# A graph attention kernel: three of sixteen tiles a chunk masked on VectorE after the exponential instead of on TensorE before it

## The reference

```python
e = (Wh @ a_src)[:, None] + (Wh @ a_dst)[None, :]
e = jnp.where(e > 0, e, ALPHA * e)             # ALPHA = 0.2
scores = jnp.where(adj > 0, e, NEG_BIG)        # -9e15 where there is no edge
attention = jax.nn.softmax(scores, axis=1)
h_prime = attention @ Wh
return jax.nn.elu(h_prime)
```

## Time and profile before

| what | value |
|---|---|
| median of 3 runs | 651.01 us (648.59 to 651.77) |
| profiled execution, its time | 648.58 us |
| profiled execution, its span | 646.5 us |
| TensorE busy | 569.7 us (88%), 3130 matmuls |
| VectorE busy | 361.8 us (56%), 490 instructions |
| ScalarE busy | 278.8 us (43%), 297 instructions |
| GpSimd busy | 31.9 us (5%), 28 instructions |
| mean granted TensorE clock | 0.952 |

### The profile page before, as it was taken

How to read it: one execution, slowest core, us unless ns; L and a number is a source line. 1 busy time by engine, 2 the same in 40 slices (tenths; PEclk the granted TensorE clock), 3 DMA queues, 4 the chain that set the end, 5 groups by cost and what they waited for, 6 DMA issues and landing times.

```text
span 646.5 us, 7470 instructions
## 1 busy us (share of the span) xinstructions
PE 569.7 (88%) x3130; PEld 195.1 (30%) x3169; DVE 361.8 (56%) x490; ACT 278.8 (43%) x297; POOL 31.9 (5%) x28
## 2 busy tenths in 40 slices
PE   5534999999999999999989998999769899999997
PEld 3301223333223344222233222245332222333332
DVE  2985766546766536766646766534989966000010
ACT  1573455434555432555532555335848666100000
POOL 0500000201000101000000000022000000000000
PEclk9556999999999999999998999999979999899999
DMA  8990000000000000000000000000000000000000
GB/s 358 368 399 11 1 0 2 1 0 1 2 1 0 1 0 3 0 1 2 0 1 1 1 0 2 0 2 1 0 1 0 2 1 0 1 1 0 1 0 33
DMA packets 3041, 19.33 MB, mean 30 GB/s; under 512 B 320, under 2 KB 320, under 8 KB 960
## 3 DMA queue, kind: packets, MB, share of 16 engines
q1 hardware_dynamic: 2864, 17.83, 6.8%
q10 hardware_dynamic: 144, 1.03, 0.5%
HBM read 18.33 MB, written 0.52 MB: 29 GB/s over the span
## 4 chain that ended last, share of the span: by engine, by line
PE 65%; DVE 21%; issue 5%; ACT 4%; DMA 2%; POOL 1%; POOLq 0%; DVEq 0%; ACTq 0%
PE PROD L653 14%; PE X L854 9%; PE S L665 9%; PE X L645 8%; PE PROD L854 7%; DVE X L1129 6%; DVE aB L1335 5%; ACT big L382 2%; DVE nadj L1238 2%; PE M L631 2%; PE X L545 2%; DMA big<-in_adjT 2%; PE S L869 2%; DVE big L1116 1%; POOL rr L319 1%
## 5 line engine op out<-in xcount | busy, mean ns | idle before, releaser
L382 ACT ACTIVATE big<-X,v 128x1024 f32<-128x1024 f32 x128 | 137.3, 1112 | 139.8 <-PE X L645 139.4
L1129 DVE SCALAR_TENSOR_TENSOR X<-wB,v,aB 128x1024 f32<-128x1024 f32 x128 | 161.5, 1289 | 59.3 <-ACT big L382 57.9
L653 PE MATMUL PROD<-big,Wh 128*64 128x512 f32 x512 | 125.9, 609 | 0.5 <-ACT big L382 0.2
L645 PE MATMUL X<-nadj,bigI 128*128 128x512 bf16 x233 | 67.3, 386 | 23.4 <-DVE X L1129 19.7
L665 PE MATMUL S<-big,onesf 128*32 128x512 f32 x512 | 68.2, 605 | 0.6 <-ACT big L382 0.6
L653 PEld LDWEIGHTS PROD<-big,Wh 128*64 128x64 f32 x512 | 30.2, 136 | 81.1 <-ACT big L382 49.8
L645 PEld LDWEIGHTS X<-nadj,bigI 128*128 128x128 bf16 x256 | 15.8, 97 | 95.8 <-DVE X L1129 72.6
L319 POOL TENSOR_TENSOR rr<-var,mhalf 128x8 f32<-128x8 f32 x8 | 17.3, 2161 | 371.5 <-DVE var L995 371.5
L854 PE MATMUL PROD<-nadj,Wh 128*64 128x512 f32 x128 | 30.3, 602 | 2.9 <-ACT nadj L473 2.9
L631 PE MATMUL M<-big,level 128*32 128x512 fp8e4 x256 | 19.8, 439 | 14.0 <-ACT big L421 11.7
L854 PE MATMUL PROD<-big,Wh 128*64 128x512 f32 x128 | 31.3, 606 | 0.7 <-ACT big L473 0.5
(11 more groups left out here) (266 smaller groups left out, 574.9 us busy)
## 6 DMA issues: line engine op xcount, KB each, us to landing
big<-in_adjT SPq DMA_DIRECT2D x13, 1024.0 KB, 7.9
aB<-in_adjT SPq DMA_DIRECT2D x3, 1024.0 KB, 8.8
cst<-in_cst ACTq DMA_DIRECT2D x1, 1008.5 KB, 5.6
x<-in_xT SPq DMA_DIRECT2D x1, 512.0 KB, 6.2
out<-x SPq DMA_DIRECT2D x2, 256.0 KB, 2.0
```

The source lines that it names most:

```text
L382: act.activation(prob[:, t % U, :], X[t % 2][:], ACT.Exp, bias=v2[l % 2][:, k:k + 1]).then_inc(p_ready, 1)
L645: last = pe.matmul(X[t % 2][:, hh * BANK:(hh + 1) * BANK], bigI[:], nadj[:, k, half_cols(c, hh)], start=False, stop=True, skip_group_check ...
L653: last = pe.matmul(PROD[c][feat(hh), :], Wh[l % 2][:, k, :], prob[:, t % U, hh * BANK:(hh + 1) * BANK], start=k == 0, stop=k == NB - 1)
L1129: dve.scalar_tensor_tensor(X[t % 2][:], wB[:, cols(c)], v8[l % 2][:, k:k + 1], aB[:, cols(c)], ALU.max, ALU.add).then_inc(x_written, 1)
```

## The change

In chunk 0 the tiles 4, 11 and 14, in chunk 1 the tiles 2, 7 and 12 of each layer (24 tiles in all) lose their `mask` on TensorE. Their exponential waits for the exponent (`x_written`) in place of the mask, and runs over unmasked values. Behind it VectorE limits the result to 3e38, multiplies it with the 8-bit adjacency and writes it back to the same buffer (`hide`, a new function, one instruction of 128x1024). In VectorE's list `hide` of tile k stands behind `exponents` of tile k+1. `products` of such a tile waits for a new semaphore, `p_hidden`, as well as for `p_ready`. Since the masks left out no longer count, `exponential` of the others waits for a number of `x_masked` that is lower by those left out so far (`hidden_by`).

```diff
+HIDE = ((4, 11, 14), (2, 7, 12))
+LARGE = 3.0e38
...
+        def hidden_by(l, c, k):
+            full = len(HIDE[0]) * (l + (1 if c else 0)) + len(HIDE[1]) * l
+            return full + sum(1 for h in HIDE[c] if h <= k)
...
             def exponential(l, c, k):
                 t = NB * (NCH * l + c) + k
-                act.wait_ge(x_masked, t + 1)
+                if k in HIDE[c]:
+                    act.wait_ge(x_written, t + 1)
+                else:
+                    act.wait_ge(x_masked, t + 1 - hidden_by(l, c, k))
...
             def mask(l, c, k):
                 t = NB * (NCH * l + c) + k
+                if k in HIDE[c]:
+                    return
                 pe.wait_ge(x_written, t + 1)
...
             def products(l, c, k):
                 t = NB * (NCH * l + c) + k
                 pe.wait_ge(p_ready, t + 1)
+                if k in HIDE[c]:
+                    pe.wait_ge(p_hidden, hidden_by(l, c, k))
...
+            def hide(l, c, k):
+                t = NB * (NCH * l + c) + k
+                dve.wait_ge(p_ready, t + 1)
+                dve.scalar_tensor_tensor(prob[:, t % U, :], prob[:, t % U, :], LARGE, adj[:, k, cols(c)], ALU.min,
+                                         ALU.mult).then_inc(p_hidden, 1)
...
                 for k in range(NB):
                     exponents(l, 0, k)
+                    if k - 1 in HIDE[0]:
+                        hide(l, 0, k - 1)
                     if 6 <= k < 10:
                         (target_first, target_second)[k % 2](l, 1, (k - 6) // 2)
...
                 for k in range(NB):
                     exponents(l, 1, k)
+                    if k - 1 in HIDE[1]:
+                        hide(l, 1, k - 1)
                     if k == 4:
                         reciprocals(l, 0)
```

More of the change, by code:

```diff
@@ L208, in program @@
         x_masked = sem("x_masked")
+        p_hidden = sem("p_hidden")
         p_ready = sem("p_ready")
```

## The result

The change makes the kernel slower: 661.39 us median (659.39 to 664.15, 4 runs) against 649.80 (648.31 to 651.77, the three runs of the table and a fourth); ratio 1.0182, 95% interval 1.0158 to 1.0207, that is +11.8 us (+10.3 to +13.5). The forecast was +10.1 us and 660, with a range of 652 to 667.

A forecast was written before the change was run, and what follows sets the result against it. TensorE was taken to set the pace, with the loop through ScalarE and VectorE nearly as long. Even tiles 0, tile 11 5.2 and tile 7 4.9 sum to +10.1 us: 660 us, range 652 to 667.

The forecast's parts named there:

- The bound: Attention tile pairs: TensorE sets the pace at 3.83 us; the loop through ScalarE and VectorE has 0.1 us to spare.
- Price of the hide: One 128x1024 hide on VectorE: 1.22 us, from the trace's fp32 operation within SBUF; 0.57 to 1.29 considered.
- rival (c): Hides on VectorE run at half throughput, 2.3 us each: +29 us, 680; chance 0.06.
- Even tiles: Chunk 0 tiles 4, 14, chunk 1 tiles 2, 12: saved mask becomes a wait for the next exponent; 0 us.
- Tile 11: Chunk 0, second of its pair: product waits for the hide, sums +1.3 us, four times, 5.2 us.
- Tile 7: Chunk 1: product waits for the hide; +1.5 us in layers 0 and 1, +0.95 in layers 2 and 3; 4.9 us.
- The sum: Whole kernel: the tile costs added together, +10.1 us, giving 660.
- (a): All 24 masks saved on TensorE, hides fit VectorE's idle time: 11.5 us less, 639.5; chance 0.10.
- the two points named: Exponent k+1 ending before products (needed 183.83, read 184.20); hide ending before its product is due (needed 182.89, read 184.13).
- (b): Even tiles save their masks after all, 7.7 us; odd tiles cost as forecast: +2.4, 653.4; chance 0.12.
- signs to look for: Profile after: 208 mask matmuls, 24 hides near 1.22 us, eight product waits, even pairs 3.83, chunk 0 +1.3 a layer.
- The granted clock: Should stay at 2.4 GHz, since it is 1.00 around the present TensorE wait of 1.31 us.

The follow-up runs named there:

- Experiment 4: Kernel after, the 24 masks left out and the hides too, so those tiles stay unmasked: 646.66 us, -3.0 us against the kernel before.
- Experiment 2: Kernel after with only tiles 4, 14 (chunk 0) and 2, 12 (chunk 1) hidden, first of their pairs: 647.82 us, -2.3 us against the kernel before.
- experiment 9: Kernel after with 36 tiles hidden, all first of their pair, TensorE's sums ahead of the one mask left: 639.03 us, -12.0 us against the kernel before.

## Why the prediction held, point by point

The forecast and its mechanism held. That 660 came so near 661.39 is in part luck: it was reckoned from 651.01, and the terms below are off in both directions.

**The bound.** TensorE looks full, but the ways through ScalarE and VectorE are as long. Experiment 4 shows that TensorE's own work is not the limit by itself (3.0 us back for 11.5 us of masks), and its timeline shows the two waits: for exponential 10 at a second tile, for exponent 15 at a first one.

**Price of the hide.** 1224 ns measured, 1.22 taken. With its 8-bit second source the hide takes as long as the fp32 operation L1352 of the earlier trace rows, 1224 ns as well. The half throughput of rival (c), about 2.3 us by the prediction's estimate, did not appear in any of the 24, which took 1215 to 1227 ns. The Trainium skill's "Vector Engine (DVE) Microarchitecture Reference", section 7, asks for it; this trace disagrees.

**Even tiles.** Forecast 0, at most 0.1 each. At tile 14 the trace has 0.43 us of waiting for the exponent where the mask was, and a pair of unchanged length. Tile 4 of layers 1 to 3 gives 0.2 us: the pair of products 2 and 3, where mask 4 stood, takes 3.65 for 3.83. Experiment 2 gives -2.3 (-3.6 to -1.0), more than those three times 0.2.

**Tile 11.** Forecast +1.3, measured +1.46 in each of the four layers. The terms that were short: from the hide's end to product 11 it is 0.14 us and not 0.05, and product 11 to mask 12 takes 1.01 and not 0.93, which was half of a pair's 1.87.

**Tile 7.** Forecast +1.5 and +0.95, measured +1.46 and +0.87, twice each.

**The sum.** 4 x 1.46 + 2 x 1.46 + 2 x 0.87 = 10.5, less 3 x 0.2 at tile 4, is 9.9; forecast 10.1. Two misses cancel here: 0.16 too little at tile 11 in each of four layers, and tile 4 put at nothing. The profiled spans differ by 12.7. From the first product to the start of the last pair of layer 3 the trace grows by 10.7 (365.65 to 376.38); of that, 0.8 lie in the first pair of layer 0; over the first two pairs the granted clock was 0.80 after and 0.88 before. The first product itself starts 3.8 us later (68.08 for 64.24), and what follows the layers takes 1.9 us less. Both lie outside the change: over all the traces of the study the first product starts between 64.0 and 68.1 us, in kernels that differ nowhere ahead of it. Whether the median's 11.8 instead of 9.9 is more than such shifts stays open; the interval begins at 10.3.

**The rivals.** (a), all masks saved, failed at the two points named. (b), even tiles that save their masks, is out by the unchanged pair. (c) is out by 1224 ns. Of the signs to look for, L657 has its 208 matmuls, and eight products wait for VectorE, 13.3 us in all. The two pairs from product 8 to product 12 take 9.21 us for 7.74, which is 1.46 a layer where I wrote 1.3. From the first product of chunk 0 to its last it is 1.3 in layers 1 and 3 and 1.2 in layer 2, as the sign has it, but only because tile 4 gives 0.2 back; in layer 0 it is 2.4, with the 0.8 of the first pair in it. The granted clock held: it is 1.00 after from 190 to 194 us, around the wait at tile 11.

## What to carry to other kernels

Before work is moved off a full engine, follow the loop through the other engines: here it was as long as the engine's own work, and leaving the work out altogether gave back a quarter. A step added between producer and consumer costs about its whole length (1.46 us for a hide of 1.22 at tile 11) unless there is a wait or other work to cover it (0.87 at tile 7 of layers 2 and 3, nothing at the first tile of a pair). So put it where the consumer comes later in line. And once an instruction is gone, see what the engine now waits for at that place and move other work there; that, with all hides at first tiles and 36 of them, turned +11.8 us into -12.0.

## What the runs showed that I had not expected

By the medians the gain of the reordered versions did not grow evenly: 24 tiles gave 5.4 us, 36 gave 12.0. The traces say otherwise. From the first product to the start of the last pair of layer 3 it takes 365.7 us before, 357.3 with 24 tiles and 354.1 with 36, which is 8.4 and 11.5 us less, 0.35 and 0.32 a tile. The medians are over other executions as well, of which there is no trace: the five runs with 24 tiles lie between 638.4 and 643.4 us, the six with 36 between 634.6 and 640.6, and what makes them differ was not tried by itself.

The gain is also not spread as I had expected. With 24 tiles chunk 1 gives 8.7 us of it, with 36 it gives 11.5, and chunk 0 in all four layers gives 0.1 either way. In chunk 0 a hidden pair of 3.44 us is paid back by one of 4.20 behind it; the hidden pairs in a row of experiment 9 (10, 12, 14) do no better there. What the larger version adds is almost all tile 10 of chunk 1: its pair takes 4.19 us for 5.33 in layer 1.
